# Batch 0 of a two-layer kernel re-planned: x loaded in eight transfers, layer 1 in products of 256 columns, y's parts read from PSUM

## What is computed

```python
# layer 0, for each batch b: W, b0 shared, mask and coeff of the batch
y = x + (x @ W0.T + b0 + (x @ (2 * mask[b] - 1)) * coeff[b])
# layer 1: W1, b1 shared, A [16, 1024] and B [1024, 16] picked by ids[b]
out = y + (y @ W1.T + b1 + (y @ A.T) @ B.T)
```

## Time and profile before

| | us |
|---|---|
| median of three runs | 409.04 (408.07 to 409.20) |
| profiled execution | 409.28 |
| its span | 407.5 |
| TensorE busy in the span | 397.8 |
| VectorE busy | 290.6 |
| ScalarE busy | 183.2 |
| GpSimd busy | 26.5 |

### The profile page before, as it was taken

How to read it: one execution, slowest core, us unless ns; L and a number is a source line. 1 busy time by engine, 2 the same in 40 slices (tenths; PEclk the granted TensorE clock), 3 DMA queues, 4 the chain that set the end, 5 groups by cost and what they waited for, 6 DMA issues and landing times.

```text
span 407.5 us, 6136 instructions
## 1 busy us (share of the span) xinstructions
PE 397.8 (98%) x2356; PEld 365.3 (90%) x2356; DVE 290.6 (71%) x375; ACT 183.2 (45%) x289; POOL 26.5 (7%) x43
## 2 busy tenths in 40 slices
PE   7999989999999999999999999999999999999995
PEld 5788878889999999999999999999999999999995
DVE  2578878866887688676887679675887679775523
ACT  3565645544435344354444444354345434353322
POOL 1234510000001000010001000010001000000000
PEclk9999999999999999999999999999999999999999
DMA  7999997159532892249622893339732693346002
GB/s 267 287 272 262 246 275 189 51 144 251 161 97 74 194 244 76 80 136 238 182 82 72 197 225 97 93 120 196 189 110 77 184 238 103 104 129 168 0 2 103
DMA packets 93488, 63.33 MB, mean 155 GB/s; under 512 B 3595, under 2 KB 90643, under 8 KB 93460
## 3 DMA queue, kind: packets, MB, share of 16 engines
q1 hardware_dynamic: 93298, 62.77, 59.2%
q10 hardware_dynamic: 162, 0.18, 0.1%
HBM read 51.39 MB, written 8.39 MB: 147 GB/s over the span
## 4 chain that ended last, share of the span: by engine, by line
PE 90%; DMA 5%; SPq 3%; issue 1%; DVE 1%; ACT 0%
PE ps L946 28%; PE ps L948 14%; PE ps L997 13%; PE ps L996 13%; PE ps L995 13%; PE ps L919 3%; DMA xraw<-in_x_dram 2%; PE ps L1018 2%; DMA xrows<-in_x_dram 2%; SPq L292 1%; PE ps L975 1%; PE ps L974 1%; PE ps L973 1%; DMA araw<-in_L_cond_lora_A_w_dram 1%; SPq L261 0%
## 5 line engine op out<-in xcount | busy, mean ns | idle before, releaser
L946 PE MATMUL ps<-xhl,whi 128*128 128x512 f32 x512 | 183.9, 397 | 0.1
L948 PE MATMUL ps<-xhl,wlo 128*128 128x256 f32 x512 | 143.2, 280 | 0.0
L946 PEld LDWEIGHTS ps<-xhl,whi 128*128 128x128 f32 x512 | 96.1, 188 | 19.6 <-issue 0.5
L997 PE MATMUL ps<-w1hi,yhl 128*128 128x344 f32 (+1 forms) x336 | 107.8, 321 | 0.0
L996 PE MATMUL ps<-w1lo,yhl 128*128 128x344 f32 (+1 forms) x336 | 107.6, 320 | 0.0
L995 PE MATMUL ps<-w1hi,yhl 128*128 128x344 f32 (+1 forms) x336 | 107.5, 320 | 0.0
L948 PEld LDWEIGHTS ps<-xhl,wlo 128*128 128x128 f32 x512 | 96.6, 189 | 0.4
L707 DVE SCALAR_TENSOR_TENSOR wlo<-wm,cs_minus,whi 128x1024 fp32r<-128x1024 f32 x62 | 80.0, 1291 | 20.7 <-ACT whi L487 20.7
L487 ACT ACTIVATE whi<-wm,cs_minus 128x1024 fp32r<-128x1024 f32 x62 | 71.5, 1153 | 39.7 <-DVE wm L700 39.7
L700 DVE SCALAR_TENSOR_TENSOR wm<-wm,cs_twice,w0t 128x1024 f32<-128x1024 int32 x62 | 80.1, 1291 | 3.9 <-DMA wm<-in_mask_Bx4096x_ik_dram 2.8
L527 ACT ACTIVATE ysum<-ps,b0col 128x256 f32<-128x256 f32 x64 | 30.4, 475 | 87.2 <-PE ps L948 87.0
(11 more groups left out here) (72 smaller groups left out, 234.2 us busy)
## 6 DMA issues: line engine op xcount, KB each, us to landing
wm<-in_mask_Bx4096x_ik_dram SPq DMA_DIRECT2D x64, 512.0 KB, 4.7
xraw<-in_x_dram SPq DMA_DIRECT2D x28, 256.0 KB, 6.3
w0raw<-in_L_cond_W_dram SPq DMA_DIRECT2D x8, 512.0 KB, 5.3
w1raw<-_L_cond_base_weight_dram SPq DMA_DIRECT2D x8, 512.0 KB, 7.7
out_dram<-zst SPq DMA_DIRECT2D x18, 172.0 KB, 2.0
bt<-bhl SPq DMA_DIRECT2D x48, 64.0 KB, 2.4
out_dram<-zst SPq DMA_DIRECT2D x8, 164.0 KB, 2.0
out_dram<-zst SPq DMA_DIRECT2D x7, 176.0 KB, 2.0
```

Of the source, the lines that this page charges most:

```text
L946: nc.tensor.matmul(ps[:, bank, :], whi[:, s, k, :], xhl[:, b % 2, k, :], start=(k == 0), stop=False, skip_group_check=True)
L948: op = nc.tensor.matmul(ps[:, bank, 0:S], wlo[:, s, k, :], xhl[:, b % 2, k, 0:S], start=False, stop=(k == KT - 1), skip_group_check=True)
L997: op = nc.tensor.matmul(dst, lo, w1hi[:, c, cols], start=False, stop=(c == KT - 1), skip_group_check=True)
```

## The change

Eight transfers load x of a batch instead of four: each brings 32 rows in full, four quarters of 256 columns into the four groups of 32 partitions. Batch 0's layer 1 runs in three products of 256 columns for each k, all summed in one place (`first_layer1`; for chunk 0 the products with x's low part can follow later). ScalarE reads that sum with the bias straight into y's high part and VectorE into its low part; the steps through ysum remain from chunk 8 on. yhl has three places in batch 0. The hand-written orders of all engines and of the loads are made anew; masks 7 and 8, A and B come in other places. The tail holds two sums instead of one. The start has two filler products fewer. Left out below are the new orders of GpSimd, ScalarE and VectorE, and the rest of TensorE's.

```diff
 
+    def y_slot(n):
+
+        return n % 3 if n < KT else n % 2
+
...
-    HELD = ((1, 2),)
+    HELD = ((1, 1), (1, 2))
...
-        yhl = sb("yhl", [P, 2, 2 * S], F32R)
-        ysum_at = nc.sbuf_base
-        ysum = sb("ysum", [P, 2, S])
+        ysum_at = nc.sbuf_base + 2 * 2 * S * 4
+        yhl = sb("yhl", [P, 3, 2 * S], F32R)
+        ysum = nc.alloc_sbuf_tensor_at("ysum", [P, 2, S], F32, offset=ysum_at)
...
-                for a in range(4):
-                    src = x[b, :, a * S:(a + 1) * S].rearrange("(n q) f -> q n f", q=Q)
-                    sp.dma_start(xraw[a * Q:(a + 1) * Q, :, :], src).then_inc(x_in, 16)
+                for r in range(S // Q):
+                    src = x[b, r * Q:(r + 1) * Q, :].rearrange("q (a f) -> a q f", f=S)
+                    sp.dma_start(xraw[:, r, :], src).then_inc(x_in, 16)
...
             sp.wait_ge(ids_in, 16)
+            names = read_names(range(0, 4))
             load_w1(0)
-            names = read_names(range(0, 4))
+            names += read_names(range(4, 8))
             load_w0(2)
+            load_a(range(4, 6))
+            load_a(range(6, 8))
+            load_b1()
             load_w1(1)
-            names += read_names(range(4, 8))
             load_mask(2)
-            load_w0(4)
+            load_b(range(0, 2))
             load_w0(3)
-            load_b1()
-            load_a(range(0, 4))
             load_w1(2)
             load_mask(3)
-            load_a(range(4, 8))
+            load_a(range(0, 2))
+            load_a(range(2, 4))
+            load_w1(3)
+            load_w0(4)
+            load_b(range(2, 4))
+            load_b(range(4, 6))
+            load_mask(4)
+            load_b(range(6, 8))
             load_w0(5)
-            load_w0(6)
-            load_w1(3)
-            load_mask(4)
             load_w1(4)
-            load_b(range(0, 8))
             load_mask(5)
             move_bias()
+            load_w0(6)
+            load_x(1)
             load_w0(7)
             load_w1(5)
-            load_x(1)
             load_mask(6)
+            load_mask(8)
             load_w1(6)
+            load_mask(7)
             load_mask(9)
-            load_mask(7)
-            load_mask(8)
+            load_bt(0)
+            load_mask(10)
             load_w1(7)
-            load_bt(0)
             load_mask(11)
-            load_mask(10)
...
-            def half_y(n):
+            def first_y_hi(n):
                 act.wait_ge(l1_done, n + 1)
                 if n == 0:
                     act.wait_ge(b0_moved, 1)
-                if n >= 2:
-                    act.wait_ge(y_lo, n - 1)
+                if n >= 3:
+                    act.wait_ge(l2_done, n - 2)
+                nc.scalar.activation(yhl[:, n % 3, 0:S], ps[:, l1_bank(n), 0:S], ACT.Identity,
+                                     bias=b0col[:, n:n + 1]).then_inc(y_hi, 1)
+
+            def half_y(n):
+                act.wait_ge(l1_done, n + 1)
+                if n == KT:
+                    act.wait_ge(l2_done, KT - 2)
+                act.wait_ge(y_lo, n - 1)
                 nc.scalar.activation(ysum[:, n % 2, :], ps[:, l1_bank(n), S:2 * S], ACT.Identity,
                                      bias=b0col[:, n % KT:n % KT + 1]).then_inc(y_half, 1)
 
             def y_parts_hi(n):
-                act.wait_ge(y_made, n + 1)
-                if n >= 2:
-                    act.wait_ge(l2_done, n - 1)
+                act.wait_ge(y_made, n - KT + 1)
+                act.wait_ge(l2_done, n - 1)
                 nc.scalar.activation(yhl[:, n % 2, 0:S], ysum[:, n % 2, :], ACT.Copy).then_inc(y_hi, 1)
...
-                dve.wait_ge(x_in, 64 * b)
+                dve.wait_ge(x_in, 128 * b)
...
+            def first_y_lo(n):
+                dve.wait_ge(y_hi, n + 1)
+                nc.vector.scalar_tensor_tensor(yhl[:, n % 3, S:2 * S], ps[:, l1_bank(n), 0:S], b0col[:, n:n + 1],
+                                               yhl[:, n % 3, 0:S].bitcast(F32), ALU.add, ALU.subtract).then_inc(y_lo, 1)
+
             def make_y(n):
-                dve.wait_ge(y_half, n + 1)
+                dve.wait_ge(y_half, n - KT + 1)
...
-                    pe.wait_ge(y_made, 1)
+                    pe.wait_ge(y_lo, 1)
...
-            def layer1(n, ks):
-                b, c = divmod(n, KT)
-                bank = l1_bank(n)
+            def first_layer1(n, ks, low=None):
+
                 s = n % WS
-                if ks[0] == 0:
+                if ks[0] == 0 and not low:
                     if n < 2:
                         pe.wait_ge(first_lo, n + 1)
                     else:
                         pe.wait_ge(w_lo, n + 1)
                     if n == 1:
                         pe.wait_ge(b0_moved, 1)
-                    elif 0 < n <= KT:
-                        pe.wait_ge(y_made, n)
-                    elif n > KT:
-                        pe.wait_ge(y_made, n - 1)
-                    if n == KT + 1:
+                    elif n > 1:
+                        pe.wait_ge(y_lo, n)
+                for k in ks:
+                    if n < 2 and k == TG and not low:
+                        pe.wait_ge(w_lo, n + 1)
+                    if n == 0 and k % TG == 0 and low:
+                        pe.wait_ge(x_lo, first_lo_split(ST - 1, k // TG))
+                    elif n == 0 and k % TG == 0:
+                        pe.wait_ge(x_hi, first_split(ST - 1, k // TG))
+                    if not low:
+                        nc.tensor.matmul(ps[:, l1_bank(n), 0:S], whi[:, s, k, :], xhl[:, 0, k, 0:S],
+                                         start=(k == 0), stop=False, skip_group_check=True)
+                    if low is not False:
+                        op = nc.tensor.matmul(ps[:, l1_bank(n), 0:S], whi[:, s, k, :], xhl[:, 0, k, S:],
+                                              start=False, stop=(low is True and k == KT - 1), skip_group_check=True)
+                    if not low:
+                        op = nc.tensor.matmul(ps[:, l1_bank(n), 0:S], wlo[:, s, k, :], xhl[:, 0, k, 0:S],
+                                              start=False, stop=(low is None and k == KT - 1), skip_group_check=True)
+                if ks[-1] == KT - 1 and low is not False:
+                    op.then_inc(l1_done, 1)
+
+            def layer1(n, ks):
+                b, c = divmod(n, KT)
+                bank = l1_bank(n)
+                s = n % WS
+                if ks[0] == 0:
+                    pe.wait_ge(w_lo, n + 1)
+                    if n == KT:
+                        pe.wait_ge(y_lo, KT)
+                    elif n == KT + 1:
                         pe.wait_ge(parts_lo, parted(number["w1", KT - 1, 0]))
-                    if c == 0 and b > 0:
+                    else:
+                        pe.wait_ge(y_made, n - 1 - KT)
+                    if c == 0:
                         pe.wait_ge(x_lo, x_split(b, 0))
                 for k in ks:
-                    if n < 2 and k == TG:
-                        pe.wait_ge(w_lo, n + 1)
-                    if n == 0 and k % TG == 0:
-                        pe.wait_ge(x_lo, first_lo_split(ST - 1, k // TG))
                     nc.tensor.matmul(ps[:, bank, :], whi[:, s, k, :], xhl[:, b % 2, k, :],
...
-                op = nc.tensor.matmul(ps[:, HB, :], at[:, c, b * 2 * R:b * 2 * R + P], yhl[:, n % 2, :],
+                op = nc.tensor.matmul(ps[:, HB, :], at[:, c, b * 2 * R:b * 2 * R + P], yhl[:, y_slot(n), :],
...
-                hi = yhl[:, c % 2, st * P:(st + 1) * P]
-                lo = yhl[:, c % 2, S + st * P:S + (st + 1) * P]
+                hi = yhl[:, y_slot(c), st * P:(st + 1) * P]
+                lo = yhl[:, y_slot(c), S + st * P:S + (st + 1) * P]
...
             idle_products(2)
+            turn_b0()
             turn_unit("x", 0, 0)
             turn_unit("x", 0, 1)
-            idle_products(2)
-            turn_b0()
             turn_unit("x", 1, 0)
             turn_unit("x", 1, 1)
             idle_products(3)
-            layer1(0, range(0, 8))
+            first_layer1(0, range(0, 4), False)
             turn_unit("w0", 1, 0)
             turn_unit("w0", 1, 1)
+            first_layer1(0, range(4, 8), False)
+            first_layer1(0, range(0, 4), True)
+            first_layer1(0, range(4, 8), True)
             turn_unit("w1", 0, 0)
             turn_unit("w1", 0, 1)
             turn_unit("w0", 2, 0)
             turn_unit("w0", 2, 1)
+            first_layer1(1, range(0, 2))
+            first_layer1(1, range(2, 4))
+            first_layer1(1, range(4, 6))
             turn_unit("w1", 1, 0)
-            layer1(1, range(0, 2))
+            first_layer1(1, range(6, 8))
+            first_layer2(0, 0, 0)
...
```

More of the change, by code:

```diff
@@ L447, in _ @@
             eye_w0(4)
+            clear_bt()
             eye_w1(3)
-            clear_bt()
+            place_a(1)
+            sort_b()
             eye_w0(5)
             eye_w1(4)
-            sort_b()
             eye_w0(6)
+            eye_w1(5)
             eye_w0(7)
```

(105 more changed lines are left out.)

91 lines of the change are left out of this document (35 added, 56 removed).

## The result

The median is 450.74 us (448.78 to 452.21, 4 runs) beside 409.12 us (408.07 to 409.42, 4 runs) for the kernel before: a ratio of 1.1019, 95% interval 1.0972 to 1.1067. The prediction was 438 us, range 410 to 462, slower with a chance of 0.81. The profiled execution has a span of 447.0 us where it was 407.5; it is the fastest of the four.

A forecast was written before the change was run, and what follows sets the result against it. TensorE's own stream, busy 98% of the span, was taken as the bound. Late x rows 25 us, batch 0 +3.8 and the tail -0.2 made +28.6 on 409.0: 437.6, say 438 us, range 410 to 462.

The forecast's parts named there:

- The number of engines: x loads: outermost count 4 in the source puts each of the eight transfers on 4 of 16 DMA engines.
- Rival (a): x loads: transfers stay as wide as before, no late rows, 405.3 us; chance 0.15.
- The rate and the late rows: x loads: 20.5 GB/s an engine, last row landing 15.0 us after the first issue, against 8.9 today.
- The stalls: TensorE before the sixth chunk's layer 1, batches 1 to 6: 25 us in sum, some 4 us a batch.
- Rival (b): x loads: narrow, but slack covers it at over 27 GB/s an engine; about 409 us; chance 0.06.
- (d): x loads: narrow and slow, 13.6 GB/s an engine, or SyncE blocked and masks late; 482 us; chance 0.05.
- Batch 0: Weights behind batch 1's rows: w1(5) late, +3.8 us in place of the plan's -3.5; bounds -3.5 to +8.
- The plan: Start and batch 0's new orders: -1.3 start, -2.7 waits gone, +0.5 given back: -3.5 us; bounds -4.5 to 0.
- HELD: Tail, two sums held: three products fewer before the end of the cover, -0.2 us; bounds -0.47 and 0.
- The start: Before layer 1: two fillers go and b0's turn moves ahead; layer 1 begins near 12.7, 1.3 us earlier.
- Products of 256 columns: Batch 0's layer 1: three take 0.35 us as the pair did, extra weight loads cost 0; upper bound 13.6 us.
- Rival (c): Batch 0's layer 1: weight loads bind the 256-column products, with x wide; 419 us; chance 0.04.

The follow-up runs named there:

- e3: The changed kernel with x in eight 128 KB transfers, each with 32 partitions outermost at both ends: 407.05 us, ratio 0.9947 to the kernel before.
- e5: The changed kernel with x in sixteen 64 KB transfers, each over 8 neighbouring partitions: 467.83 us, ratio 1.1364 to the kernel before.
- f2: The changed kernel with x in sixteen 64 KB transfers of 2 column quarters x 32 rows, outermost count 2: 524.82 us, ratio 1.2781 to the kernel before.
- e1: The changed kernel with x in the four transfers of before and nothing else altered: 407.09 us, ratio 0.9951 to the kernel before.
- e4: The changed kernel with only batch 1's rows in the eight narrow transfers, later batches in four wide ones: 412.73 us, ratio 1.0060 to the kernel before.
- e7: The changed kernel with x in four transfers and one sum held in the tail instead of two: 407.01 us, ratio 0.9913 to the kernel before.
- e6: The changed kernel plus 18 filler products of 512 columns before the sixth chunk's layer 1, batches 1 to 6: 441.07 us, ratio 1.0750 to the kernel before.
- g1: The changed kernel with x in sixteen transfers, each over 8 partitions spaced four apart: 429.99 us, ratio 1.0521 to the kernel before.

## Why the prediction came out as it did

The direction, the mechanism and the main term were right; the size was 12.7 us short. That it lies inside the range is partly luck: the range reached to 462 for rows that land later than the sum had them, and they did not. What was missing was another term, the clock, for which the range had nothing.

**The number of engines: right, and now shown for sides that differ.** The queue that carries x is q1. It had 93298 packets before and has 93074 after, 224 fewer, and the page's packets under 512 B fell by the same 224, from 3595 to 3371. Counted as completions, one for each engine of a transfer: the 28 old transfers with 16 completions each were 448, the 56 new ones with 4 each are 224. e3 (56 with 16) and e5 (112 with 8) should both have 448 more than before and have: 93746. f2 (112 with 2) should have as many as after, and has: 93074. So in all these runs the number of engines is the outermost count of the source, up to 16: 2, 4, 8 and 16. In none was the destination the narrower side, so that half of the rule is untested here. This is the rule of the Trainium skill, DMA: Bandwidth & Descriptors, section "Why a DMA increments its semaphore by 16 and not by 1", and these counts agree with it. Rival (a) falls with it.

**The rate and the late rows: right, by errors that nearly cancel.** The sum took 20.5 GB/s an engine and a landing 15.0 us after the first issue. It was 24 GB/s with x alone in flight, and 15.6 us to VectorE's turn. The rate was too low and the start too early, as the prediction had seen for today's transfers: the first packets of x are through 2.6 to 3.0 us after the first issue, while a mask still shares the engines; SyncE now needs 7.80 us for its eight issues, not 4 (presumably the last ones stood until the four engines had room; no run tests that). The Trainium skill, DMA: Bandwidth & Descriptors, Specifications, gives some 27 GiB/s (29 GB/s) an engine; the fastest stretch of 1 us in any trace here moved 420 GB/s over 16 engines, 26 each (e1, from 7 us on), and with x alone none moved more than 24; the estimate of 11 us to the landing that came from it was 4.6 us short. The stalls: 25 us forecast, 25.3 measured, six times some 4 us. (VectorE's own wait for x was 44.8 us, more than the 25 to 40 named as a sign.) Rival (b) falls, and (d) too: four engines moved x at 24 GB/s each and not at 13.6, and VectorE's waits for masks behind x stayed small (3.4 us in sum, 2.8 before).

**Batch 0: 3 to 6 us, forecast 7.3.** The forecast was +3.8 in place of -3.5. Narrow against wide, chunk 9's layer 1 starts at 84.38 in the changed kernel, at 80.38 in e1, 81.16 in e3: 3.2 to 4.0 us in an execution whose clock did not fall in batch 0. Where it did, in e4, the cost was 5.7 us against e7. The late piece is the one it named: the first unit of w1(5) ran at 56.32 (forecast 58.3, before 53.20) after a wait of 2.99 us.

**The plan: about -2.1 us, forecast -3.7 with HELD.** e1 and e3 are 0.5% under the kernel before; e7, on another chip, 0.9% with an interval that overlaps theirs. The start is worth another amount in each execution: layer 1 began at 13.39 in the changed kernel, 13.26 in e3, 12.85 in e7 and 11.63 in e1 (forecast 12.7, before 14.03). The reason is in the pace of TensorE. The sixteen transposes of the rows took 3.68 us in the changed kernel, 0.23 us each, and 2.08 in e1. A stretch reads PEclk 1.00 in both, but only because the trace's clock records begin later: at 13.8 us in the changed kernel and 8.5 in e1, each with the full clock. At these times the pace doubles (products of 256 columns start 0.21 us apart until 13.81 and 0.12 after it), so up to there TensorE ran, it seems, at the lower of its two levels. The waits for the second B unit, A and the copy of W0 went (2.7 us, but e7 still waits 0.4 for A) and others came: one for W1's low half (1.0 us after, 1.1 in e1, 0.7 in e7), and the waits for pieces of W0 grew in e1 by 1.2. So 1.1 to 2.3 us were given back instead of 0.5; this is where the plan fell short.

**Products of 256 columns: 0, as forecast.** They are 0.12 us apart in the changed kernel's timeline, with a new weight for each:

```profile
14.16 0.28 PE L953 MATMUL ps<-xhl,wlo 128*128 128x256 f32 x1
14.28 0.28 PE L947 MATMUL ps<-xhl,whi 128*128 128x256 f32 x1
14.40 0.28 PE L953 MATMUL ps<-xhl,wlo 128*128 128x256 f32 x1
```

Rival (c) falls. HELD's -0.2 is too small to be shown: e7's profile has a wait of 0.6 us for h that e1 has not, and its span is 0.4 us longer, but the medians agree.

**The term that failed: what a stall costs.** The prediction priced each of the six stalls at its own length and had no term for the clock behind it. Spans: 447.0 - 407.5 = 39.5 us. Of these 25.3 are the waits and 1.2 is batch 0 (84.38 against 83.23 for chunk 9). The 13.0 that remain, 2.2 a batch, are products at half the pace after the wait: counted in the trace, TensorE worked 25.5 us at 0.50 there, which costs 12.8. e6 shows it by an edit: fill the wait, and 9.7 to 11 us go though the rows are as late. So in this kernel a wait of 4 us costs 6. With this term the forecast would have been 438 + 13 = 451; that this meets the measured 450.7 so well owes something to errors that cancel: batch 0 cost 1.2 us over before and not 3.8, and the profiled execution, from which the 13 is read, is 1.5 us or more faster than the other three.

## What to carry to other kernels

Before a transfer is cut anew, count the outermost dimension of both sides: in these runs the smaller one, up to 16, was the number of DMA engines that worked on it (the source's in each), and 4 in place of 16 makes everything behind it on those engines late too. Eight transfers of the same 128 KB, with 32 partitions outermost, cost nothing (e3). Price a stall of TensorE that grows from nothing to some microseconds at more than its length: look in the rows at what the granted clock does behind the waits that the kernel has, and if it has none that long, keep a term for it. Don't take the length of a wait for the whole story: here waits of 1.8 and 2.0 us (g1) were followed by the lower clock and one of 3.0 us (batch 0 of the changed kernel) was not. e1 and e3 are the best versions found, both 0.5% under the kernel before; e7 can't be told from them.

## What the runs showed of the hardware that was not expected

- The granted clock fell to 0.50 during five of the six waits of about 4 us, and 0.15 us after the other, the fourth (at 269.8 us), and stayed there after work had begun again (110 to 116 us above). In e1, without these waits, every slice of the page reads 9, a mean of 1.00.
- Shorter waits can do it too, and don't always: in g1 the clock fell behind waits of 1.81, 3.02 and 1.98 us and not behind 1.86, 1.93 and 2.06 us. A wait of 3.0 us in batch 0 was followed by 0.50 in e6 and by 1.00 in the changed kernel.
- Eight engines whose transfers write 8 neighbouring partitions moved no more than four engines in the change's transfers: 93 to 99 GB/s, 12 an engine, with 1 KB packets of 120 ns. With the 8 partitions four apart the packets took 46 ns.
- An issue on SyncE took 0.5 us for wide transfers (e3, 4.00 for 8), 0.97 for those on four engines, 1.2 for two (19 for 16), 0.36 for 8 neighbouring partitions and 0.72 for 8 spread ones. For two and four engines, engines that are full would explain it; for the last pair nothing here does.
